# Queries and keys as two float32r limbs in 32-row array tiles, attention unrolled

## The reference

```python
x = x + attn_a(layernorm(x), Wq, Wk, Wv)
x = x + ffn(layernorm(x), router, bias, w1, w2, w3, sw1, sw2, sw3)
x = x + attn_b(layernorm(x), w_qkv, w_out, b_out)
x = x + ffn(layernorm(x), ...)
# attn_a: 16 heads of 8 features
scores = einsum('bqhd,bkhd->bhqk', Q, K) / sqrt(8)
alpha = softmax(scores)                    # over all 1024 keys
alpha = where(causal, alpha, 0)            # masked AFTER the softmax
Y = einsum('bhqk,bkhd->bqhd', alpha, V)
# attn_b: rotary q and k, no mask, softmax, times v, times w_out, + b_out
# ffn: softmax router, the best 2 of 8 experts, each silu(x@w1)*(x@w3)@w2, and one shared
```

## Time and profile before

| | us |
|---|---|
| median of 3 runs | 2334.4 |
| lowest and highest | 2331.25, 2337.49 |
| profiled execution, first to last instruction | 2335.9 |
| of it attention a, first exponent to last | 140 to 952 |
| of it attention b | 1295 to 2095 |

### The profile page before, as it was taken

The page is one execution under the profiler, slowest core; times in us unless marked ns, Lnnn a source line. Parts: engine busy times, 40 slices in busy tenths (PEclk is TensorE's granted clock), DMA queues, the critical chain, the costliest instruction groups (busy, mean ns, idle before and its releaser), DMA issues. The chain is left out here.

```text
span 2335.9 us, 45054 instructions
## 1 busy us (share of the span) xinstructions
PE 2088.4 (89%) x15817; PEld 905.2 (39%) x16064; DVE 1747.2 (75%) x2442; ACT 1402.6 (60%) x2380; POOL 557.9 (24%) x579
## 2 busy tenths in 40 slices
PE   2689999999899999689975999999999999995999
PEld 1223333333333332478840223223222232225888
DVE  7687777778777873478887888878777888807777
ACT  1247776777677778422231677767777777782222
POOL 5234444454444455300052200000000000003000
PEclk9679999999999999689985899999999999996999
DMA  3510000100000000000024001100000010000000
GB/s 90 169 49 24 25 24 28 36 33 24 25 24 25 24 2 2 1 25 0 1 72 134 30 24 35 35 26 24 24 25 25 28 37 8 2 2 0 10 14 14
DMA packets 78586, 69.96 MB, mean 30 GB/s; under 512 B 40240, under 2 KB 73648, under 8 KB 73648
## 3 DMA queue, kind: packets, MB, share of 16 engines
q1 hardware_dynamic: 78384, 67.20, 8.9%
HBM read 47.52 MB, written 18.87 MB: 28 GB/s over the span
## 5 line engine op out<-in xcount | busy, mean ns | idle before, releaser
L308 DVE TENSOR_REDUCE b_negmax<-ps_two 128x1 f32<-128x1024 f32 x512 | 624.8, 1224 | 155.0 <-PE ps_two L300 154.8
L308 DVE TENSOR_REDUCE a_negmax<-ps_two 128x1 f32<-128x1024 f32 x512 | 617.3, 1222 | 154.8 <-PE ps_two L300 153.3
L731 ACT ACTIVATE at_probs<-ps_one 128x512 f32<-128x512 f32 x992 | 580.4, 597 | 243.3 <-PE ps_one L863 159.5
L300 PE MATMUL ps_two<-kx,qx 96*128 96x512 bf16 x2048 | 651.7, 402 | 79.6 <-DVE ap_rest L445 18.5
L731 ACT ACTIVATE bt_probs<-ps_one 128x512 f32<-128x512 f32 x992 | 588.4, 597 | 190.2 <-PE ps_one L863 156.9
L863 PE MATMUL ps_one<-qx,kx 128*128 128x512 bf16 x1746 | 670.9, 388 | 15.6 <-issue 8.1
L863 PEld LDWEIGHTS ps_one<-qx,kx 128*128 128x128 bf16 x1984 | 189.0, 96 | 539.5 <-issue 281.2
L841 PE MATMUL ps_sum<-bt_probs,vg 128*9 128x256 f32 x4096 | 322.3, 387 | 7.7 <-ACT bt_probs L731 0.6
L300 PEld LDWEIGHTS ps_two<-kx,qx 96*128 96x128 bf16 x2048 | 196.2, 100 | 236.8 <-DVE b_negmax L308 47.3
L687 POOL TENSOR_TENSOR at_pdiag<-at_probs,causal 128x512 f32<-128x512 f32 x128 | 162.5, 1269 | 359.6 <-ACT at_probs L731 359.6
L1172 ACT ACTIVATE xn<-ps_two 128x512 f32<-128x512 f32 x144 | 86.0, 597 | 234.8 <-PE ps_two L1141 234.8
(11 more groups left out here) (147 smaller groups left out, 1606.9 us busy)
## 6 DMA issues: line engine op xcount, KB each, us to landing
qx<-qk_parts SPq DMA_DIRECT2D x96, 192.0 KB
kx<-qk_parts SPq DMA_DIRECT2D x96, 192.0 KB
qk_parts<-ap_parts SPq DMA_DIRECT2D x24, 256.0 KB, 2.8
qk_parts<-bp_parts SPq DMA_DIRECT2D x24, 256.0 KB, 2.6
vg<-v_rows SPq DMA_DIRECT2D x32, 128.0 KB
x<-in_x SPq DMA_DIRECT2D x4, 512.0 KB, 6.1
v_rows<-ap_vbuf SPq DMA_DIRECT2D x8, 256.0 KB, 2.7
v_rows<-bp_vbuf SPq DMA_DIRECT2D x8, 256.0 KB, 2.6
```

Of the source, the lines that this page charges most:

```text
L300: last = pe.matmul(m.ps_two[:, slot, half * CHUNK:(half + 1) * CHUNK], m.qx[0:MAXROW, g, hh, i * P:(i + 1) * P], m.kx[0:MAXROW, g, hh, hal ...
L308: dve.tensor_reduce(sc.negmax[:, parity, hh * NT + i:hh * NT + i + 1], m.ps_two[:, slot, :], AX.X, ALU.max, negate=True).then_inc(sc.read, 1)
L731: act.activation(probs[:, jj % 4, hh, half * CHUNK:(half + 1) * CHUNK], exponent_bank(n_left, hh, half), ACT.Exp, scale=SCALE).then_inc(ex ...
```

## The change

**Operands.** q and k are split into two float32r limbs. The stored rows are three products (high.high, high.low, low.high), 24 rows per head. Head h of a group lies at partitions 32h to 32h+23 of `qx` and `kx` (4 slots, one per group), and the maximum's two limbs at rows 32h+24 and 32h+25. A score matmul contracts 24 rows, an exponent matmul 26, each in one 32-row tile of the array. `load_group` has 8 DMAs of 24 rows of 4 KB, the maxima 8 of one row each. V is not stored: ACT copies it into `vg` in place, 4 copies a chunk. `project` holds no scores and no loads of groups any more; both stand at the start of `attend`.

**Units.** A score unit is now two heads by 512 keys (two matmuls into two banks, from two row tiles); one DVE maximum gives two columns, and `combine` takes the smaller of the two halves. **Exponents** go round three banks, the third in `ps_sum`. **Weighing** takes a block of one key tile by 512 queries, four heads, 512 columns, once every two steps; one `ps_sum` bank holds the sums, so it is copied and cleared after each half. The pair additions on POOL are gone. Scores run 44 units ahead of the exponents. All loops over groups and chunks are unrolled.

```diff
-    m.qx = sb("qx", [P, NG, GH, S], BF16)
-    m.kx = sb("kx", [P, NG, GH, S], BF16)
+    m.qx = sb("qx", [P, SLOTS, S], F32R)
+    m.kx = sb("kx", [P, SLOTS, S], F32R)
...
-            pool.memset(m.kx[:, :, :, :].bitcast(F32), 0.0).then_inc(cleared, 1)
+            pool.memset(m.kx[:, :, :].bitcast(F32), 1.0)
...
+            for chunk in range(CHUNKS):
+                for limb, limb_done in ((0, high), (1, low_done)):
+                    sp.wait_ge(limb_done, chunk + 1)
+                    for c, order in enumerate(((0, 0, 1), (0, 1, 0))):
+                        for row in range(PRODUCTS):
+                            if order[row] == limb:
+                                sp.dma_start(m.qk_rows[b, c, row, :, h * CHUNK:(h + 1) * CHUNK]...)
+            for slot in range(SLOTS):
+                sp.wait_ge(stored[slot], DMA * 2 * PRODUCTS * (CHUNKS // SLOTS))
...
-            for v in range(STEPS):
-                take_max(dve, m, sc, 0, v // NT, v % NT, v % 2, v)
...
+UNITS = NT * HALVES * 2
+BLOCKS = HALVES * NT
+LEAD = 12
+PROB_SLOTS = 4
+E_BANKS = 3
...
+            def copy_sums(n, half):
+                act.wait_ge(pv_done, BLOCKS * n + NT * (half + 1))
+                act.activation(sums[:, half * CHUNK:(half + 1) * CHUNK], acc, ACT.Copy).then_inc(acc_copied, 1)
+            for blk in range(GROUPS * BLOCKS):
+                if blk >= PROB_SLOTS:
+                    act.wait_ge(pv_done, blk - PROB_SLOTS + 1)
+                for k, h in enumerate((2, 3, 0, 1)):
+                    count = blk * GH + k
+                    act.wait_ge(e_filled, count + 1)
+                    act.activation(probs[:, blk % PROB_SLOTS, h, :], e_banks[count % E_BANKS], ACT.Exp, scale=SCALE
+                                   ).then_inc(exp_done, 1)
+                    if k == 1 and blk >= NT + 1 and (blk - 1) % NT == 0:
+                        copy_sums(*divmod((blk - 1) // NT - 1, HALVES))
...
+            def score(unit, slot, count):
+                if count >= 2:
+                    pe.wait_ge(taken, count - 1)
+                for bank, h in enumerate(heads_of(u)):
+                    rows = slice(TILE_ROWS * h, TILE_ROWS * h + ROWS)
+                    last = pe.matmul(m.ps_two[:, slot, bank * CHUNK:(bank + 1) * CHUNK],
+                                     m.qx[rows, n % SLOTS, i * P:(i + 1) * P],
+                                     m.kx[rows, n % SLOTS, half * CHUNK:(half + 1) * CHUNK], start=True, stop=True)
+            def exponents(blk, k):
+                h, count = (2, 3, 0, 1)[k], blk * GH + k
+                if count >= E_BANKS:
+                    pe.wait_ge(exp_done, count - E_BANKS + 1)
...
+            def weigh(blk):
+                pe.wait_ge(exp_done, GH * (blk + 1))
+                if j == 0 and blk:
+                    pe.wait_ge(acc_copied, blk // NT)
...
+            for step in range(GROUPS * UNITS):
+                blk, part = divmod(step, 2)
+                ring(step)                       # score unit, turned maxima or sums
+                for k in range(2):
+                    exponents(blk, part * 2 + k)
+                if part and blk:
+                    weigh(blk - 1)
```

More of the change, by code:

```diff
@@ L126, in over_chunks @@
 def over_chunks(eng, body, lead=0, start=0):
[L129 to L140, removed]
+    for t in range(-lead, CHUNKS):
+        body(t, t, lambda k: 0 <= t + k < CHUNKS)
 def moment_semaphores(nc, ctx, tag):
@@ L263, in norm_pe_turn, with project @@
     last.then_inc(s.turned, 1)
[L266 to L309, removed]
-def project(nc, m, layer, later, group_loaded, sc):
+LOADS = 2 * GH
+def project(nc, m, layer, later):
     rope = layer == "b"
@@ L816, in turn_sums @@
                                         m.ident[:, :])
[L817 to L833 removed]
+                last.then_inc(filled, 1)
@@ L838, in weigh @@
-                    for hh in range(GH):
-                        w = m.w01[:, :] if kind == "ones" else m.vg[:, g, j, hh:hh + GH * (rows - 1) + 1:GH]
-                        src = pdiag[:, jj % 2, hh, :] if kind == "diagonal" else probs[:, jj % 4, hh, q0:q1]
-                        last = pe.matmul(m.ps_sum[32 * hh:32 * hh + rows, half, q0 - half * CHUNK:q1 - half * CHUNK],
-                                         w, src, start=clears and k == 0,
-                                         stop=jj == NT - 1 and k == len(pieces) - 1, skip_group_check=True)
@@ L892, in _ @@
[L892 to L900 removed]
+                        pe.wait_ge(masked, diagonals(blk) + 1)
+                    width = HD if kind == "diagonal" else HD + 1
@@ new lines, in weigh @@
+                    for h in range(GH):
+                        w = m.w01[:, :] if kind == "ones" else m.vg[:, b * NT + j, g * GH + h, 0:width]
+                        src = (pdiag[:, diagonals(blk) % 2, h, :] if kind == "diagonal" else
+                               probs[:, blk % PROB_SLOTS, h, q0 - half * CHUNK:q1 - half * CHUNK])
+                        last = pe.matmul(acc[32 * h:32 * h + width, q0 - half * CHUNK:q1 - half * CHUNK], w, src,
+                                         start=j == 0 and k == 0, stop=j == NT - 1 and k == len(pieces) - 1,
+                                         skip_group_check=True)
@@ L1263, in build @@
         m = allocate(nc, ctx)
-        group_loaded = {layer: [ctx.enter_context(nc.semaphore(f"{layer}_group_loaded{g}")) for g in range(NG)]
-                        for layer in "ab"}
-        scores = {layer: Scores(nc, ctx, layer) for layer in "ab"}
         expert_loads = [
```

591 lines of the change are left out of this document (231 added, 360 removed).

## The result

The changed kernel takes 2791.38 us (median of 4 runs, 2778.78 to 2824.14), the kernel before 2334.45 beside it: ratio 1.194, interval 1.190 to 1.198. It is a fifth slower; forecast were 2262.

What follows compares the result with a forecast made beforehand. PE's own work bound attention before, the ring would after: 2335.9 - 42 (b) - 26 (a) - 11 (steps without scores) + 10 (start) = 2267, with loop ends and profiling off 2262 us; range 2215 to 2310.

Steps and rivals of the forecast that it cites:

- the ring: Loop of waits per attention block, through three exponent banks and four exponents before the weighing: 2.75 us, against 3.06.
- rival C: PE's clock falls in attention: block 4.2 us; near 2980 us for good, near 2500 for a third of the time; 8%.
- The two score loads: In the ring, two score loads stand ahead of a block's first exponent: 2 x 0.12 = 0.24 us.
- E2's load to its exp: In the ring, from the load of a block's first exponent, E2, to the start of its exp: 0.52 us.
- E1's load to the weighing: In the ring, from the load of the fourth exponent, E1, to the first load of the weighing: 0.40 us.
- Rival B: Row tiles' loads overlap too, 0.02 instead of 0.12 us: 0.20 less per block with scores, 2168 us; 17%.
- The copies of the sums: First weighing of a half waits for ACT's copy of the one bank: 0.75 us, twice a group, 1.5.
- Rival A: Row tiles don't overlap, the ring takes 2.97 us: 2365 us, slower than before by 1.3%; 13%.
- D: DVE's lateness from division, moments and combine reaches the ring: +77 us at most, 2339, no change; 5%.
- E: ACT and DVE bound attention, DVE's work 40.5 us a group: near 2035 us; 2%.
- The slower load of float32r: PE's weight load takes 0.19 us against 100 ns for bfloat16; 0.09 more where a load is waited for.
- The start of attention: Group 0 loads behind a barrier, 12 to 14 us; 44 units precede the first exponent, not 40: +5 a layer, +10.

## Why the prediction was wrong

- **The step that failed is the clock.** The forecast took every term of the ring at 2.4 GHz and gave the fall, rival C, 8%. It measured 0.66 in a and 0.52 in b, and that cost 564 us. C's own sums were right: 4.2 us a block at 1.2 GHz, measured 4.13 in b; near 2500 for a third of the time and near 2980 for good, measured 2791 with 368 of 470 blocks low. Wrong was the condition. I weighed it by PE's share of time and mentioned the "quarter or half of the rows in use" without a price. The sentence against it, that PE would be busy all the time at 1.2 GHz and the clock had risen in that state at the start of each attention, compared a PE with 96 and 128 rows to one with 24 to 26: b had 976 of 1100 us busy and 0.52, and the kernel before with 32 rows 896 of 900 and 0.52. With 64-row tiles in the same order the clock was 0.99. Few rows were what it took, but not the only condition: with the weighing cut in two the same rows had 0.97 in a. The Trainium skill (TensorE: Matmul & The Clock Gate, "Part 1: The HAM clock gate") sets the clock by how busy PE has been; by busy time alone these 900 us should have run at 2.4 GHz, so here the measurement decides, and the rows count as well.
- **The block at 2.4 GHz** was forecast at 2.75 and was 2.68 in b, 2.87 in a (forecast: 9216 columns a group, so 0.1 more; in a it is 2.69 without a diagonal tile and 2.90 with one). Terms were off both ways and partly cancel, which is luck. The two score loads cost 0.01, not 0.24; E2's load to its exp took 0.63, not 0.52; from the end of the exp to E1's load, which the sum left out, it is 0.05 (536.06 to 536.11); E1's load to the weighing 0.42, not 0.40. The weighing with its change was 0.97 at 2.4 GHz (1725.78 to 1726.75, with 64-row tiles), against 0.99.
- **Rival B's mechanism was true**, loads of different row tiles run together. The Trainium skill (TensorEngine Tiling (Array Packing), "Tiling Modes") says so, and the trace agrees: two loads and two matmuls in the time of one. In the ring it saved 0.23 (B had 0.20), and the other terms above took 0.16 of it back in sum: 0.07 us a block are left.
- **The copies of the sums** were sized at 0.75 us a half. With 64-row tiles at 2.4 GHz PE waited 31 times for them in b, at most 0.6, 17.9 us in all.
- **Rival A fell** by the same rows. **D and E** did not decide. The waits in b (us in total, times, longest) have DVE waiting for PE's scores:

```profile
DVE bt_negmax L596 <- PE ps_two L668: 423.9, 233, 2.5
```

- **The slower load of float32r** was right in size (0.18 to 0.19 against 0.10), hidden in 32-row tiles and in the open with full rows, 0.15 a half block.
- **The start of attention** was sized too long by 14 us in a and by 2 in b.

What stays open: at what mix of rows and share of time the clock turns. The runs show both levels for the same code (32 rows with the split weighing, 64 rows one at a time). For 64 rows one at a time a gap of PE of over 3 us tips it down; what lifts it again, and what tips it with 32-row tiles, where the longest gap before a fall in the middle of an attention is 1.3 us, they don't show.

## What to carry to other kernels

Before cutting a matmul's contraction into small row tiles, look at how many rows of the array stay in use at once, and at the clock of every stretch where few are: here the tiles' overlap was worth 0.4 us of a 3 us block (3.12 to 2.68) and the lost clock cost 1.5. Keep 128 rows at work with tiles that run side by side, zeros in the unused rows if need be. And where the matmuls between two long pieces of work need more banks than there are, as the four exponents with three banks here, cut the long piece, since moving it only moves the wait. That pays only where this loop is the bound: with full rows it cost 45 us.

## What the runs showed of the hardware

- The granted clock by rows in use, in attention: 96 and 128 rows 0.99; 128 rows, three quarters of one operand zero, 0.99 to 1.00; two tiles of 64 at once 0.99 to 1.00; tiles of 64, the two heads of a pair in the same one, float32r, 0.99; 64 rows one at a time, bfloat16, either level; 24 and 26 rows 0.52 to 0.66, and 0.53 to 1.00 with the weighing cut in two; 32 rows one at a time 0.52.
- Either level can hold for hundreds of us in unchanged code, so times of a kernel near the edge spread: 2838.64 to 3066.47 for 64 rows, 2807.54 to 2945.18 for the changed kernel with its weighing moved, against 0.1 to 0.4% for the kernels that hold 2.4 GHz.
- Behind a gap of PE of 3.2 to 3.9 us the clock was low for less than 7 us with 96 and 128 rows, and for 27 to 396 us with 64 rows one at a time.
- Loads and matmuls of four different row tiles start within 0.01 us of each other. At 1.2 GHz a float32r load of 128 columns takes 0.28 instead of 0.18 and a matmul of 512 columns 0.79 instead of 0.49, drain included.
